# Weight sums and their low parts moved from GpSimd to VectorE, layer norms of the steps spread over two steps, deferred phase reordered, in a two-layer macaron block on one Trainium2 core

## The reference

```python
x = x + 0.5 * L0_ffn(layernorm(x))      # quant:  x @ Wq.T + bias
x = x + L0_attn(layernorm(x))           # conv:   S4 kernel, causal, over the features
x = x + 0.5 * L0_ffn(layernorm(x))
x = x + 0.5 * L1_ffn(layernorm(x))      # (silu(x @ Wg.T) * (x @ Wu.T)) @ Wd.T, 512 -> 1376 -> 512
x = x + L1_attn(layernorm(x))
x = x + 0.5 * L1_ffn(layernorm(x))
```

## Time and profile before

| what | value |
|---|---|
| median of three runs | 993.14 us (990.47 to 993.26) |
| profiled execution, own time | 996.58 us |
| its span, first to last instruction | 994.8 us |
| mean granted clock of TensorE | 0.976 |
| busy PE, DVE, ACT, POOL | 903.6, 642.2, 410.9, 634.4 us |
| DMA over the span | 59.67 MB, 60 GB/s |

### The profile page before, as it was taken

The page is one execution under the profiler, slowest core; times in us unless marked ns, Lnnn a source line. Parts: engine busy times, 40 slices in busy tenths (PEclk is TensorE's granted clock), DMA queues, the critical chain, the costliest instruction groups (busy, mean ns, idle before and its releaser), DMA issues.

```text
span 994.8 us, 11946 instructions
## 1 busy us (share of the span) xinstructions
PE 903.6 (91%) x4088; PEld 731.2 (74%) x4088; DVE 642.2 (65%) x1021; ACT 410.9 (41%) x650; POOL 634.4 (64%) x835
## 2 busy tenths in 40 slices
PE   3989997599889988899999888999999789999998
PEld 2767986478667866788878666788877667888876
DVE  7787865556656685676667665666667647566664
ACT  3533544523343344343443462443443543333332
POOL 5964475866666657566667566666677574666633
PEclk9999998899999999999999999999999899999999
DMA  9200000002212222121121222121121231322214
GB/s 334 86 1 1 1 1 1 0 22 64 56 39 64 64 67 71 42 64 43 53 64 43 64 64 73 34 64 43 54 65 39 71 113 44 106 63 64 64 45 146
DMA packets 25228, 59.67 MB, mean 60 GB/s; under 512 B 2640, under 2 KB 2896, under 8 KB 25168
## 3 DMA queue, kind: packets, MB, share of 16 engines
q1 hardware_dynamic: 25168, 58.91, 19.5%
HBM read 54.70 MB, written 4.19 MB: 59 GB/s over the span
## 4 chain that ended last, share of the span: by engine, by line
PE 55%; POOL 19%; DVE 12%; ACT 6%; issue 6%; DMA 3%; SPq 0%; POOLq 0%; DVEq 0%; ACTq 0%
PE front L1291 10%; PE front L1293 10%; PE front L1292 10%; PE acc L1245 5%; PE acc L1247 5%; PE acc L1246 4%; POOL down_lo L569 3%; POOL row_operands_lo L516 3%; POOL w_and_weight_operands_lo L559 3%; PE front L440 2%; PE acc L1185 2%; POOL rstd L422 2%; PE acc L1184 2%; PE acc L1183 2%; DVE w_and_weight_operands_lo L554 2%
## 5 line engine op out<-in xcount | busy, mean ns | idle before, releaser
L1291 PE MATMUL front<-row_operands_hi,weight_operands_hi 128*128 128x512 f32 x616 | 247.4, 402 | 23.1 <-DVE snapshots L1084 12.1
L1293 PE MATMUL front<-row_operands_hi,w_and_weight_operands_lo 128*128 128x512 f32 x616 | 243.5, 395 | 0.0
L1292 PE MATMUL front<-row_operands_lo,weight_operands_hi 128*128 128x512 f32 x616 | 243.3, 395 | 0.0
L569 POOL TENSOR_TENSOR down_lo<-raw_down,down_hi 128x512 fp32r<-128x512 f32 x88 | 131.8, 1499 | 141.6 <-ACT down_hi L564 133.0
L1245 PE MATMUL acc<-down_hi,hidden_hi 128*128 128x512 f32 x352 | 143.0, 406 | 27.1 <-DVE hidden_lo L1118 16.2
L1291 PEld LDWEIGHTS front<-row_operands_hi,weight_operands_hi 128*128 128x128 f32 x616 | 117.6, 191 | 58.6 <-issue 28.0
L1084 DVE TENSOR_TENSOR snapshots<-front,snapshots 128x512 f32<-128x512 f32 x132 | 91.1, 690 | 81.5 <-PE front L1293 80.1
L1247 PE MATMUL acc<-down_hi,hidden_lo 128*128 128x512 f32 x352 | 138.8, 394 | 0.0
L1246 PE MATMUL acc<-down_lo,hidden_hi 128*128 128x512 f32 x352 | 138.8, 394 | 0.0
L1293 PEld LDWEIGHTS front<-row_operands_hi,w_and_weight_operands_lo 128*128 128x128 f32 x616 | 117.5, 191 | 25.6
L1292 PEld LDWEIGHTS front<-row_operands_lo,weight_operands_hi 128*128 128x128 f32 x616 | 117.6, 191 | 23.3
(11 more groups left out here) (159 smaller groups left out, 1585.1 us busy)
## 6 DMA issues: line engine op xcount, KB each, us to landing
raw_weights<-wgu SPq DMA_DIRECT2D x44, 512.0 KB, 3.5
raw_down<-wdown SPq DMA_DIRECT2D x88, 256.0 KB, 2.7
x_rows<-x_in SPq DMA_DIRECT2D x3, 1024.0 KB, 13.6
out<-x_rows SPq DMA_DIRECT2D x3, 1024.0 KB, 5.3
x_rows<-x_in SPq DMA_DIRECT2D x2, 512.0 KB, 5.6
q_raw<-qweight SPq DMA_DIRECT2D x4, 256.0 KB, 7.1
out<-x_rows SPq DMA_DIRECT2D x4, 256.0 KB, 2.0
omega_terms<-omega_in SPq DMA_DIRECT2D x1, 768.0 KB, 11.1
```

Source lines behind the costliest of these rows:

```text
L569: nc.gpsimd.tensor_tensor(WDl[:, q % WD_RING, :], WDr[:, q % WD_RING, :], WDh[:, q % WD_RING, :].bitcast(F32), ALU.subtract).then_inc(wd_r ...
L1291: T.matmul(o, wh, xh, start=(j == 0), stop=False)
L1292: T.matmul(o, wh, xl, start=False, stop=False)
L1293: last = T.matmul(o, wl, xh, start=False, stop=(j == 1))
```

## The change

Four things change.

1. In each step the four weight sums and all low parts are made by DVE. The high and low parts and the raw blocks lie in one tensor `W` in a new block order, raw blocks in the place of the low parts, so that a low part is written over the raw block. DVE's order is: C11, sums S1 and S3, U2, sums S2 and S4, T_SUM, U3, C22, three low parts (768, 768 and 256 columns), then as before. The first sum waits for the DMA of the raw blocks. ACT makes three high parts (768, 768, 256) instead of two (768, 1024).
2. `STATS_OF_STEP` takes the place of `LN_OF_STEP`: unit 0 makes one layer norm's statistics in each of steps 1 to 8; units 1 and 2 as before. The rstd sequence and the norm of a step's items are done one step later, on POOL right behind second_hidden, on ACT between the raw and the sums' high parts.
3. In the opening phase the eight `prep` items stand one behind each of quants 7 to 14.
4. In the deferred phase ACT makes pair copies in passes 0, 2, 4, 6 and the sums' high parts in passes 1, 3, 5, 7; DVE makes pair sums in passes 0, 2, 4, 6 and pair lows in 1, 3, 5, 7. The order of PE and POOL there is as it was.

```diff
-A11, A12, A22, S1, S2, S3, S4 = range(7)
-A21_RAW = 0
+S4, A22, A11, A12, S2, S1, S3 = range(7)
+A21_RAW = S4
...
-    after = {8: (0, 1), 10: (2, 3), 11: (4, 5), 12: (6, 7)}
+    after = {UTILES - 1 + p: (p,) for p in range(UTILES)}
...
+    for _p in range(UTILES):
+        _f = 7 + _p // 2 if EMBEDDED[_u] else 1 + _p
+        STATS_OF_STEP[_u][_f].append(UNIT_ITEMS[_u] + EMBEDDED[_u] + _p)
...
+        def weight_sums_a(dve, k):
+            dve.wait_ge(w_in[k % 2], 16 * (k // 2 + 1))
+            nc.vector.tensor_tensor(raw_block(k, S1), raw_block(k, A21_RAW), raw_block(k, A22), ALU.add).then_inc(w_step, 1)
+            nc.vector.tensor_tensor(raw_block(k, S3), raw_block(k, A11), raw_block(k, A21_RAW), ALU.subtract
+                                    ).then_inc(w_step, 1)
+
+        def weight_sums_b(dve, k):
+            dve.wait_ge(w_step, 4 * k + 2)
+            nc.vector.tensor_tensor(raw_block(k, S2), raw_block(k, S1), raw_block(k, A11), ALU.subtract
+                                    ).then_inc(w_step, 1)
+            dve.wait_ge(w_step, 4 * k + 3)
+            nc.vector.tensor_tensor(raw_block(k, S4), raw_block(k, A12), raw_block(k, S2), ALU.subtract
+                                    ).then_inc(w_step, 1)
+
+        def weight_lows(dve, k):
             dve.wait_ge(w_step, 4 * k + 4)
+            for i, (first, last) in enumerate(((A22, A12 + 1), (S2, S3 + 1), (S4, S4 + 1))):
+                dve.wait_ge(w_hi, 3 * k + i + 1)
+                nc.vector.tensor_tensor(flat(W, k, LO, first, last), flat(Wr, k, LO, first, last),
+                                        flat(W, k, HI, first, last).bitcast(F32), ALU.subtract).then_inc(w_ready, 1)
...
                     if f:
                         second_hidden(k - 1)
-                    if k + 1 < STEPS:
-                        weight_sums(pool, k + 1)
+                    for n in STATS_OF_STEP[u].get(f - 1, ()):
+                        rstd_step(pool, n)
                     down_weight_lo(pool, q + 1)
-                    if k + 1 < STEPS:
-                        weight_sum_lo(pool, k + 1)
-                    for n in LN_OF_STEP[u][f]:
-                        rstd_step(pool, n)
                 second_hidden(FT * u + FT - 1)
+                for n in STATS_OF_STEP[u][FT - 1]:
+                    rstd_step(pool, n)
...
                     if k + 1 < STEPS:
-                        weight_raw_hi(act, k + 1)
-                        weight_sum_hi(act, k + 1)
+                        weight_hi_raw(act, k + 1)
+                    for n in STATS_OF_STEP[u].get(f - 1, ()):
+                        norm_step(act, n)
+                    if k + 1 < STEPS:
+                        weight_hi_sums(act, k + 1)
                     down_weight_hi(act, q + 1)
...
                 silu(FT * u + FT - 1, g1, C12)
-                if u + 1 < UNITS:
-                    pair_copies(act, BLK * (u + 1))
                 second_hidden_hi(u, 0)
+                for n in STATS_OF_STEP[u][FT - 1]:
+                    norm_step(act, n)
                 for j in range(FT):
                     q = PASSES * u + FT + j
-                    if u + 1 < UNITS and j in (0, 2, 4, 6):
-                        sums_hi_step(act, BLK * (u + 1) + j // 2)
                     if q + 1 < UNITS * PASSES:
                         down_weight_hi(act, q + 1)
-                    if u + 1 < UNITS and j in (1, 3, 5):
-                        pair_copies(act, BLK * (u + 1) + (j + 1) // 2)
+                    if u + 1 < UNITS and j in (0, 2, 4, 6):
+                        pair_copies(act, BLK * (u + 1) + j // 2)
+                    if u + 1 < UNITS and j in (1, 3, 5, 7):
+                        sums_hi_step(act, BLK * (u + 1) + j // 2)
...
-                if u + 1 < UNITS:
-                    pair_sums(dve, BLK * (u + 1))
                 for r in range(BLK):
                     ffn_update(u, 0, r)
-                if u + 1 < UNITS:
-                    pair_lows(dve, BLK * (u + 1))
-                for j in range(1, FT):
-                    hidden_lo(q1 + j, H1[:, j, :])
-                    if u + 1 < UNITS and j in (2, 4, 6):
+                for j in range(FT):
+                    if u + 1 < UNITS and j in (0, 2, 4, 6):
                         pair_sums(dve, BLK * (u + 1) + j // 2)
+                    if u + 1 < UNITS and j in (1, 3, 5, 7):
                         pair_lows(dve, BLK * (u + 1) + j // 2)
+                    if j + 1 < FT:
+                        hidden_lo(q1 + j + 1, H1[:, j + 1, :])
```

More of the change, by code:

```diff
@@ L187, in build @@
         OPl, _ = sb("row_operands_lo", [P, 7, 2, D], F32R)
-        Wh, _ = sb("weight_operands_hi", [P, 2, 7, 2, P], F32R)
-        Wl, wl_at = sb("raw_and_weight_operands_lo", [P, 2, 8, 2, P], F32R)
-        WDh, _ = sb("down_hi", [P, WD_RING, D], F32R)
-        WDl, wdl_at = sb("down_lo", [P, WD_RING, D], F32R)
+        W, w_at = sb("weight_operands", [P, 2, 2, 7, 2 * P], F32R)
+        WD, wd_at = sb("down_weights", [P, WD_RING, 2, D], F32R)
         Hh, r_at = sb("hidden_hi", [P, 2, D], F32R)
@@ L557, in weight_sum_lo, with flat, weight_hi @@
-        def weight_sum_lo(pool, k):
-            pool.wait_ge(w_sum_hi, k + 1)
-            nc.gpsimd.tensor_tensor(flat(Wl, k, 1 + S1, 2 + S4), flat(Wr, k, 1 + S1, 2 + S4),
-                                    flat(Wh, k, S1, S4 + 1).bitcast(F32), ALU.subtract).then_inc(w_sum_ready, 1)
+        HI, LO = 0, 1
+        def flat(t, k, part, first, last):
+            return t[:, k % 2, part, first:last, :].rearrange("p o c -> p (o c)")
+        def weight_hi(act, k, first, last):
+            if first == A22:
+                act.wait_ge(w_in[k % 2], 16 * (k // 2 + 1))
+            else:
+                act.wait_ge(w_step, 4 * k + 4)
+            nc.scalar.activation(flat(W, k, HI, first, last), flat(Wr, k, LO, first, last), ACT.Copy).then_inc(w_hi, 1)
@@ L866, in _ @@
                         xt_hi_step(act, embedded_item(u, f - 1))
-                    for n in LN_OF_STEP[u][f]:
-                        norm_step(act, n)
                     act.wait_ge(first_made, k + 1)
@@ L1076, in _ @@
                     strip(n - 13)
+                if n == PRE - 6:
+                    weight_sums_a(dve, 0)
                 if n == PRE - 5:
-                    weight_raw_lo(dve, 0)
+                    weight_sums_b(dve, 0)
+                if n == PRE - 3:
+                    weight_lows(dve, 0)
             def add(k, product, read, out, other):
@@ L1137, in _ @@
                         update_step(dve, embedded_item(u, f - 2))
-                    for n in LN_OF_STEP[u][f]:
+                    for n in STATS_OF_STEP[u][f]:
                         stats_step(dve, n)
@@ L1288, in product @@
                 for j in range(2):
-                    wh, wl = Wh[:, k % 2, a, j, :], Wl[:, k % 2, 1 + a, j, :]
+                    wh, wl = (W[:, k % 2, part, a, j * P:(j + 1) * P] for part in (HI, LO))
                     xh, xl = OPh[:, b, j, :], OPl[:, b, j, :]
```

114 lines of the change are left out of this document (49 added, 65 removed).

## The result

The kernel after takes 962.91 us (median of 4 runs, 960.23 to 967.23), the kernel before on the same chip 992.51 (4 runs). The ratio is 0.9709, 95% interval 0.967 to 0.9748, so it is faster, and the forecast of 964 us is 1 us off. The profiled execution took 963.32, with a span of 961.5; the one of before had 994.8, so 33.3 us are to be found.

The account below looks back on a forecast made before the run. TensorE, busy 91%, was taken as the bound, with only idle and lower-clock time to win. Terms -13 - 9.5 - 6.2 - 1.8 + 0.8 = -29.7 off 996.6 gave 966.9, less 3.4 to the median: 964 us, range 944 to 984.

Parts of the forecast that it names:

- The rule of serial ports: All stages: a DVE operation with two SBUF operands and a GpSimd one run one after the other; overlaps priced as serial waits.
- Weights in a step: Steps: weight sums and lows moved to DVE; gain 1.8 us in unit 3, nought in units 1 and 2, first steps +0.8.
- the residue of 0.3 us a step: Unit 3 steps: GpSimd's sum_lo delayed the product into g0, 12.5 us instead of 12.3; removing it gains 1.8 over ten steps.
- the embedded steps: Steps of units 1 and 2, 14.6 us each: change taken as nought for both units, bounds -3 and +16.
- part 2: Layer norms in unit 0's steps, spread to one a step: -9.5 us, bounds -13.5 and -5.
- First step of unit 0: First steps of units: lows end at 11.35 instead of 11.15 us, costing 0.2 each, +0.8 for four.
- Norms in unit 0: Unit 0 steps: rstd chain goes, DVE late instead, 12.8 us a step; six steps 76.8 instead of 87.2, sum -9.5.
- Opening: Last part of the opening phase: GpSimd stays the limit, 44 us instead of 57, so -13; ends -20 and -5.
- Deferred phases: Deferred phases: reordered queues give -3.2 us in unit 0 and -1.5 each in units 1 and 2, sum -6.2.
- rival (b): Opening and deferred phases: norms not the point, waits only exchanged, -5 and +4 instead of -13 and -6.2; 982 us, chance 0.19.
- Rival (a): Steps: DVE becomes their bound, sums at 0.75 us each, weight work 7.4 not 3.6; about 1040 us, chance 0.09.

Follow-up runs that it names:

- experiment 2: Kernel before with only the layer norms spread: one per step in unit 0, rstd and norm a step later; 972.62 us, ratio 0.9776.
- experiment 9: Kernel before with norms spread over two steps and one preparation after each of the last quants, no weights or deferred change; 966.99 us, ratio 0.9727.
- experiment 10: Kernel after with GpSimd's deferred reorder and wait, its opening low parts one item later, and first-step x_rows additions behind hidden_lo; 946.11 us, ratio 0.9507.
- Experiments 4: Kernel before with only the deferred-phase reorder on ScalarE and VectorE, GpSimd's order left; 994.26 us, ratio 1.0001.
- experiment 7: Kernel after without its deferred-phase reorder, ScalarE and VectorE in the order of before; 964.45 us, ratio 0.9692.
- experiment 6: Kernel after with GpSimd's pair low parts in odd deferred passes, waiting until DVE's next hidden_lo has gone first; 949.60 us, ratio 0.9553.
- experiment 3: Kernel before with only the preparations moved, one behind each of quants 7 to 14; 989.17 us, ratio 0.9941.

## Why the prediction was right, and where not

The total is right to 1 us, and part of that is luck. The prediction is a gain of 29.7 us, taken off a profiled execution that lay 3.4 us above its median. The two medians are indeed 29.6 apart, but the two profiled executions, in which the terms can be followed, are 33.3 apart. There the terms miss by up to 3 us each: the opening brought less than forecast, the steps of all units more, and these cancel in part. By the steps of the prediction:

- **The rule of serial ports** held: low parts of 768 columns at 1.22 us on average, 0.95 undisturbed, additions from PSUM at 0.69. The price taken for a sum of 256 columns from SBUF, 0.42, was measured at 0.42 to 0.45 on average.
- **Weights in a step.** The low parts end at 11.0, walked 11.0 to 11.3. Unit 3 gained 3.8 us to its end, not 1.8: the residue of 0.3 us a step went, and brought 2.0, as forecast. The other 1.8 is step 1 alone (14.1 us instead of 16.0), where TensorE waits 1.9 us before and 1.6 after, and ran behind that wait at the lower clock only before: the matmuls of 512 columns in seven rows are shown with 0.63 us instead of 0.39. In the embedded steps nought was taken for units 1 and 2; they gained 1.4 and 1.9. That is a balance: the norms alone gained 4.1 and 2.6 there in experiment 2 (2.6 and 2.7 in experiment 9), which the prediction had not seen at all (part 2 priced unit 0 only), and the weights took 1.1 and 0.8 back. First step of unit 0: +0.7 instead of +0.2.
- **Norms in unit 0.** -11.2 against -9.5. The mechanism forecast, DVE late with the sum that M1 wants, is what the rows show; its size was taken as 0.5 us a step and is 0.3 (12.53, not 12.8). That the norms are what held these steps is now shown: without the norms' part the steps stay long (108.8), without the weights' part they don't (102.1).
- **Opening.** -10.2 in the stretch against -13: 46.8 us, not 44. The step that failed is that GpSimd stays the limit, at 9.7 per two quants and two preparations, with a share of its idle time added. Two and two take 10.9 (the gaps of TensorE at 157.42, 168.30 and 179.18 have one pattern), and GpSimd is busy 32.6 of 46.8 us. Postponing its longest operation there (experiment 10) gained nothing: the waits of 1.71 us became 1.54, like the others, and a wait of 1.6 for another row came in. So another ring sets it. The norm of a tile behind the copy of the transposes (xt_hi) on ScalarE, which waits for TensorE's transposes, fits the rows (TensorE waits 9.7 us for the norms, ScalarE 15.2 for the transposes), but no run isolated it. I had also missed that 6 us of this would come as clock.
- **Deferred phases.** The sum, -6.2, was met by -1.5, -2.3 and, in unit 2's stage, -2.7; that it fits is luck, as the terms in it don't. In unit 0 the -3.2 walked is the idle time that went; the clock, which the prediction charged only to units 1 and 2, took 1.7 back there. In unit 1 it was the other way about: idle time should have fallen by 3.5 and the clock taken 2, and idle time stayed while the clock gave 2.15. The cause was not the one named first. Experiments 4 and 7 put the reorder at nothing; in units 1 and 2 it is the norms that left the way of hidden_hi in step 10 (70.0 and 69.9 with the norms alone). The series that the prediction names as what comes (high part, sums_lo, a locked-out hidden_lo, down_lo) is right to the row, and it eats what the reorder brings: rival (b) described this place correctly, though not the total.
- **Rival (a)**, the slower side, had its mechanism right in unit 0: DVE does set these steps, by 0.3 us each, and one more operation in each is paid in full there, with 10 to 13 us over the span. But its price of 0.75 for a sum is not what the chip showed: the four sums ran at 0.42 to 0.45.

What stays open: which ring sets the opening, and whether experiment 6 needs the reorder.

## What to carry to other kernels

Two changes that shorten one chain don't add up: run each part alone and one pair before paying for both; here the costlier part, the weights on DVE, brought 2 to 3.5 us once the cheap one was in. An empty list of waits doesn't mean that nobody waits: here 0.3 us a step lay under the shown tail of a matmul, and the length of a step against that of its matmuls, or one operation added, brings it out. Where two engines lock each other out of SBUF, the order in which they start decides: let the short operation that TensorE waits for go first and have the engine with the long one wait for it, even if it idles. And a reorder on two of the three engines that share a chain measured nothing here; with the third engine's order changed too the time fell by 15 us, though which of the edits were needed was not taken apart.

## What the runs showed that I had not expected

A gap in TensorE's work of 2 us and more often cost nearly twice its length, but not always. Windows of the kernel after around its two gaps in unit 0's deferred phase (2.28 us up to 346.95, 2.17 us up to 363.64); the granted clock is the third value from the right:

```profile
341.00:345.00 4.00, 3.67 (x21) 2.84 (x19) 3.22 (x4) 3.28 (x7) 2.26 (x1) 1.00 0.23 70
346.90:352.00 5.10, 5.05 (x18) 4.08 (x19) 2.59 (x5) 1.96 (x3) 4.10 (x3) 0.67 0.01 3
352.00:358.00 6.00, 6.00 (x31) 4.99 (x30) 2.69 (x6) 2.94 (x8) 1.96 (x2) 1.00 0.31 87
...
363.60:370.00 6.40, 6.36 (x21) 5.11 (x22) 3.53 (x6) 2.21 (x3) 4.75 (x3) 0.73 0.10 24
```

The mean clock is 1.00 up to each gap, 0.67 and 0.73 in the five to six microseconds behind it, and 1.00 again after, so part of these ran at the lower of the two levels, 1.2 instead of 2.4 GHz: the pass of twelve matmuls behind the first gap took 4.4 us (346.95 to 351.36), where 2.7 is usual, so the first gap cost 1.7 us more than itself. Gaps of 0.37 us at 335.33 and of 1.5 to 1.7 us in the opening had no such trail; there the clock is 1.00 throughout. Nor does every long gap have one. Here is the same wait of 2.56 us, for hidden_lo in front of the deferred phase, in unit 1 (up to 540.09) and in unit 2 (up to 745.20) of the kernel after:

```profile
540.10:546.00 5.90, 5.90 (x28) 4.89 (x29) 3.75 (x5) 2.97 (x7) 4.08 (x10) 1.00 0.17 50
...
745.20:751.00 5.80, 5.80 (x18) 4.63 (x19) 3.94 (x5) 2.87 (x6) 3.98 (x10) 0.71 0.07 13
```

Of its seven gaps above 2 us between 300 and 800 us, five have the trail. It also explains a spread between kernels that are alike in a stage: unit 2's steps take 133.7 us in experiment 7 and 135.2 in the kernel after, and step 1 (15.4 and 17.0) makes all of it, behind a gap of 2.4 us that has a trail only in the latter. What decides between the two cases no run here shows. In experiment 6, where the waits of unit 0's stretch sum to 1.9 us, the clock is 1.00 too. And in the opening, spreading the preparations alone (experiment 3) brought the clock between 150 and 200 us to 1.00, where the kernel before and the weights' part alone had 0.86.
